# A bidirectional Mamba scan on one core: decays of the state pairs made further ahead, and projections moved to other steps

## The reference, cut to what matters

```
u, z = split(x @ in_w.T)
u    = silu(conv4(u) + conv_b)            # four taps over time
dbc  = u @ xproj_w.T
dt   = softplus(dbc[:, :64] @ dt_w.T + dt_b)
B, C = dbc[:, 64:80], dbc[:, 80:96]       # 16 states
A    = -exp(A_log)
h_n[t] = exp(dt[t] * A_n) * h_n[t-1] + dt[t] * u[t] * B_n[t]     # for each state n
y[t]   = sum over n of h_n[t] * C_n[t]  +  u[t] * D
out    = (y * silu(z)) @ out_w.T
```

## Time and profile before

| | us |
|---|---|
| median of 3 runs | 1427.17 (1426.55 to 1429.71) |
| the profiled execution | 1421.74 |
| its span | 1419.9 |
| busy: TensorE, VectorE, ScalarE, GpSimd | 1265.3, 1081.2, 966.3, 978.3 |
| TensorE's granted clock, mean | 0.987 of full speed |
| Mamba block, end of its last sum | about 870 |

### The profile page before, as it was taken

How to read it: one execution, slowest core, us unless ns; L and a number is a source line. 1 busy time by engine, 2 the same in 40 slices (tenths; PEclk the granted TensorE clock), 3 DMA queues, 4 the chain that set the end, 5 groups by cost and what they waited for, 6 DMA issues and landing times.

```text
span 1419.9 us, 28744 instructions
## 1 busy us (share of the span) xinstructions
PE 1265.3 (89%) x10310; PEld 977.1 (69%) x10310; DVE 1081.2 (76%) x1813; ACT 966.3 (68%) x1662; POOL 978.3 (69%) x604
## 2 busy tenths in 40 slices
PE   6698899899899898989989877998998999998995
PEld 2566766766677676676667765568997666666993
DVE  6688898888888988889888985433335788987775
ACT  5788887887878888888788794224555555454443
POOL 2688988898898898889889882621333466565673
PEclk9999999999999999999999989999999999999998
DMA  6544545445444544444544434231214200002233
GB/s 215 142 120 129 173 140 162 144 131 141 144 143 123 144 170 145 150 137 130 163 144 139 130 120 178 74 94 42 85 55 149 92 2 1 1 17 59 76 100 104
DMA packets 175036, 163.52 MB, mean 115 GB/s; under 512 B 114416, under 2 KB 139504, under 8 KB 165184
## 3 DMA queue, kind: packets, MB, share of 16 engines
q1 hardware_dynamic: 170128, 151.87, 34.8%
q0 software_dynamic: 4768, 9.81, 2.1%
HBM read 147.11 MB, written 20.52 MB: 118 GB/s over the span
## 4 chain that ended last, share of the span: by engine, by line
PE 60%; DVE 17%; ACT 12%; issue 8%; DMA 1%; POOL 1%; DVEq 1%; SPq 0%; POOLq 0%; ACTq 0%
DVE hh L900 9%; PE pa L511 9%; PE py L530 8%; PE pq L416 6%; ACT da L722 3%; PE bank L1591 2%; PE bank L1601 2%; PE bank L1587 2%; PE pr L2045 2%; PE pr L2248 2%; PE pr L2059 2%; PE bank L1507 2%; DVE hh L910 2%; PE pq L426 2%; PE pq L465 2%
## 5 line engine op out<-in xcount | busy, mean ns | idle before, releaser
L1065 POOL TENSOR_TENSOR hc<-hh,cs 128x1024 f32<-128x1024 f32 x256 | 598.1, 2370 | 116.3 <-DVE hh L900 107.4
L900 DVE TENSOR_TENSOR_SCAN hh<-da,st,pa 128x512 f32<-128x512 f32 x288 | 349.5, 1262 | 48.8 <-ACT da L722 29.2
L511 PE MATMUL pa<-dg,dtut 64*128 64x128 f32 x3072 | 236.3, 287 | 83.4 <-DVE hh L900 73.2
L511 PEld LDWEIGHTS pa<-dg,dtut 64*128 64x128 f32 x3072 | 201.0, 190 | 144.4 <-issue 138.5
L530 PE MATMUL py<-ident,hc 128*128 128x128 f32 x2048 | 271.9, 277 | 5.5 <-POOL hc L1065 3.1
L530 PEld LDWEIGHTS py<-ident,hc 128*128 128x128 f32 x2048 | 228.1, 142 | 53.3 <-issue 30.9
L722 ACT ACTIVATE da<-dt,w 128x512 f32<-128x512 f32 x384 | 251.5, 710 | 0.2
L900 DVE TENSOR_TENSOR_SCAN hh<-da,pa 128x512 f32<-128x512 f32 x96 | 111.5, 1205 | 25.3 <-PE pa L511 14.0
L416 PE MATMUL pq<-xn,w 128*128 128x512 f32 x248 | 124.2, 625 | 2.8 <-ACT xn L766 2.8
L910 DVE TENSOR_TENSOR_SCAN hh<-pa,st,hh 128x512 f32<-128x512 f32 x96 | 116.0, 1260 | 1.7 <-ACT pa L727 1.7
L1717 POOL DMA_INDIRECT ytoken<-ysort,token x39 | 39.9, 1023 | 103.1 <-ACT ysort L1649 102.5
(11 more groups left out here) (340 smaller groups left out, 2615.1 us busy)
## 6 DMA issues: line engine op xcount, KB each, us to landing
cs<-bcrows SPq DMA_DIRECT2D x64, 1024.0 KB, 5.0
dg<-blocks SPq DMA_DIRECT2D x96, 256.0 KB, 5.1
bs<-bcrows SPq DMA_DIRECT2D x32, 256.0 KB, 3.4
brow<-bcrows SPq DMA_DIRECT2D x32, 256.0 KB, 5.3
blocks<-bcrows SPq DMA_DIRECT2D x384, 1.0 KB, 3.2
xsorted<-in_pads SPq DMA_DIRECT2D x13, 387.0 KB, 6.3
rot<-in_rot SPq DMA_DIRECT2D x4, 1024.0 KB, 5.0
wx<-in_l_w SPq DMA_DIRECT2D x4, 1024.0 KB, 11.2
```

The costliest lines, as they stand in the source:

```text
L511: mm = pe.matmul(pa[i % SLOTS + r].rearrange("p (j k n) -> p k n j", n=2, k=4)[:, kt, :, :], dtut[rows, kt, h * P:(h + 1) * P], dg[k % DGS ...
L900: v.tensor_tensor_scan(hh[(NS * m + nj) % HHS][:, h, :], da[q % DAS][:, :], inflows, 0.0 if first else st[:, m % 2, nj, h:h + 1], ALU.mult ...
L1065: g.tensor_tensor(hc[s % HCS][:, :, :], hh[s % HHS][:, :, :], cs[j % 2][:, s % CG, :].unsqueeze(1).broadcast_to([P, HF, CH]), ALU.mult).th ...
```

## The change

The `da` ring gets eight tiles instead of six. The decays of the pairs are counted by a semaphore of their own, `s_da`, so that they may be made in another order than the other slots; it takes over the semaphore `s_zero` of a later phase, whose two waits there are raised by the 384 pair decays (`zero0 = UNITS * 4 * len(PAIRS)`; those lines are left out below). `elsewhere` therefore leaves the items "flow" out of the count of `s_slot`.

`DECAYS_FIRST` and `DECAYS_LATE` say at which step ScalarE makes which decays, ahead of or behind `prep`. dt is projected at steps 4 and 5 instead of 5 and 6, with its relu and abs at 5 and 6. The sigmoid comes at the end of step 6, the squares at 7, 8 and 10. The output projection of the late kind comes at steps 0 and 1 instead of 1 and 2. The taps of u go one each at steps 8 to 11 for half 0, and three at 12 and one at 13 for half 1; before they were two each at 10 to 13. `D * u` is made at step 5 and added with state 3, which is in step 7. The inflows at steps 10 and 11 stand ahead of the sum as in other steps.

```diff
--- before.py
+++ after.py
@@ -32,11 +32,13 @@
 BY_G = (0, 1)
 BY_V = (4, 13)
 SPREAD_AT = (0, 8)
+DECAYS_FIRST = {0: (1,), 1: (2, 3), 3: (4,), 6: (7,), 7: (10,), 8: (11,), 9: (12,), 11: (14,), 12: (13, 15), 15: (16,)}
+DECAYS_LATE = {4: (5, 6), 6: (8, 9)}
 BY_P = tuple(n for n in range(NS) if n not in BY_G + BY_V)
 PAIRS = tuple(BY_P[i:i + 2] for i in range(0, len(BY_P), 2))
 DGS = 3
 HQ = P // 2
-SLOTS, DAS, BG, BVS = 4, 6, 2, 2
+SLOTS, DAS, BG, BVS = 4, 8, 2, 2
 HHS, HCS = 6, 4
 LAG = 4
 
@@ -216,7 +219,7 @@
             s_slot, s_taken = sem("slot_filled"), sem("slot_taken")
             s_dtu = sem("dtu_made")
             s_b, s_db, s_gdb = sem("b_rows_in_psum"), sem("inflow_by_vector"), sem("inflow_by_gpsimd")
-            s_brow = s_back
+            s_brow, s_da = s_back, s_zero
             s_pin = sem("inflow_by_tensor")
             s_dout = sem("diagonals_out")
             s_dg = [sem(f"diagonals_in{i}") for i in range(DGS)]
@@ -303,11 +306,11 @@
 
                 handed_items = handed()
                 turn = {item: i for i, item in enumerate(handed_items)}
-                by_tensor = [item[0] == "y" for item in handed_items]
+                elsewhere = [item[0] in ("y", "flow") for item in handed_items]
 
                 def slot_count(i):
 
-                    return i + 1 - sum(by_tensor[:i + 1])
+                    return i + 1 - sum(elsewhere[:i + 1])
 
                 def dt_count(m):
 
@@ -381,7 +384,7 @@
 
                     return s // NS * len(by) + sum(n < s % NS for n in by)
 
-                DD_AT = 9
+                DD_AT = 3
                 EARLY = (13, 14, 15)
 
                 def turned_count(m, h):
@@ -472,17 +475,17 @@
                         if m < UNITS:
                             if n == 3:
                                 x_project(m)
-                            if n in (5, 6):
-                                dt_project(m, n - 5)
-                        if m >= 3 and late_out(m - 3) and n in (1, 2):
-                            out_project(m - 3, ((0, 1), (2, 3))[n - 1])
+                            if n in (4, 5):
+                                dt_project(m, n - 4)
+                        if m >= 3 and late_out(m - 3) and n in (0, 1):
+                            out_project(m - 3, ((0, 1), (2, 3))[n])
                         if m >= 2 and m - 2 < UNITS - 1 and not late_out(m - 2) and n in (8, 9):
                             out_project(m - 2, ((0, 1), (2, 3))[n - 8])
                         if m + 1 < UNITS:
-                            if n in (10, 11):
-                                u_half(m + 1, 0, ((0, 1), (2, 3))[n - 10])
+                            if n in (8, 9, 10, 11):
+                                u_half(m + 1, 0, (n - 8,))
                             if n in (12, 13):
-                                u_half(m + 1, 1, ((0, 1), (2, 3))[n - 12])
+                                u_half(m + 1, 1, ((0, 1, 2), (3,))[n - 12])
                         if m < UNITS and n in (14, 15):
                             z_half(m, n - 14)
 
@@ -574,7 +577,7 @@
                             turn_dtu(m, 1)
                         if n == NS - 1 and m + 1 < UNITS:
                             turn_dtu(m + 1, 0)
-                        if s + 1 < STEPS and by_pe(s + 1) and n not in (LAG + 1, 10, 11):
+                        if s + 1 < STEPS and by_pe(s + 1) and n != LAG + 1:
                             inflow(s + 1)
                         if s in (1, 2, 3):
                             pe.wait_ge(s_xt, s + 1)
@@ -590,8 +593,6 @@
                                 inflow(s + 1)
                         if n != LAG and s >= LAG:
                             add_up(s - LAG)
-                        if n in (10, 11):
-                            inflow(s + 1)
                         if n not in (LAG + 1, *EARLY):
                             prep(m + 1, n)
                     for s in range(STEPS - LAG, STEPS):
@@ -678,10 +679,8 @@
                         if m < UNITS:
                             if n == 4:
                                 keep_rows(m)
-                            if n in (6, 7):
-                                relu_abs(m, n - 6)
-                            if n == 7:
-                                sigmoid(m)
+                            if n in (5, 6):
+                                relu_abs(m, n - 5)
                         if m + 1 < UNITS and n == 14:
                             keep_pre(m + 1, 1)
                         if m < UNITS and n == 15:
@@ -690,11 +689,11 @@
                             keep_pre(m, 3)
                         if n == 1:
                             silu(m)
-                        if n == 12:
+                        if n == 5:
                             u_times_d(m - 1)
                         if m < UNITS:
-                            if n in (8, 9, 10):
-                                square(m, n - 8)
+                            if n in (7, 8, 10):
+                                square(m, (7, 8, 10).index(n))
                             if n == 11:
                                 relu_again(m)
                         if m + 1 < UNITS and n == 11:
@@ -719,7 +718,7 @@
                                     k0, j0 = (q - DAS) // 4, (q - DAS) % 4
                                     act.wait_ge(s_taken, turn["flow", k0, j0 // 2, j0 % 2] + 1)
                                 a = W_A + h * NS + PAIRS[k % len(PAIRS)][j]
-                                act.activation(da[q % DAS][:, :], dt[m % 2][:, h, :], ACT.Exp, scale=wd[m % 2][:, a:a + 1]).then_inc(s_slot, 1)
+                                act.activation(da[q % DAS][:, :], dt[m % 2][:, h, :], ACT.Exp, scale=wd[m % 2][:, a:a + 1]).then_inc(s_da, 1)
                         else:
                             for h in range(HF):
                                 i = turn["step", s, h]
@@ -802,13 +801,11 @@
                     for s in range(STEPS):
                         if s % NS == LAG and s >= NS:
                             keep_sum(s // NS - 1)
-                        ahead = s + 1 < STEPS and by_pe(s + 1) and BY_P.index((s + 1) % NS) % 2 and (s + 1) % NS < 10
-                        if s + 1 < STEPS and not ahead:
-                            decays(s + 1)
+                        for n in DECAYS_FIRST.get(s % NS, ()):
+                            if s // NS * NS + n < STEPS:
+                                decays(s // NS * NS + n)
                         if s == 0:
                             keep_dtu(0, 0)
-                        if s % NS == PAIRS[0][0] - 1:
-                            decays(s + 2)
                         if s >= 3 and s % 2:
                             keep_states(s - 3)
                         if s == 1:
@@ -821,14 +818,16 @@
                         if s == 4:
                             decay_rates(1)
                         prep(s // NS + 1, s % NS)
+                        for n in DECAYS_LATE.get(s % NS, ()):
+                            decays(s // NS * NS + n)
+                        if s % NS == 6 and s // NS + 1 < UNITS:
+                            sigmoid(s // NS + 1)
                         if s % NS == 0:
                             keep_dtu(s // NS, 1)
                         if s % NS in SPREAD_AT:
                             spread_b(s // NS * NS + BY_V[SPREAD_AT.index(s % NS)])
                         if s % NS == NS - 1 and s + 1 < STEPS:
                             keep_dtu(s // NS + 1, 0)
-                        if s % NS in [own[0] - 1 for own in PAIRS[1:] if own[1] < 10]:
-                            decays(s + 2)
                         if s // NS == UNITS - 1:
                             n = s % NS
                             if n == 1:
@@ -895,7 +894,7 @@
                             v.wait_ge(s_pin, 2 * k + h + 1)
                             for j, nj in enumerate(own):
                                 i, q = turn["flow", k, h, j], 4 * k + 2 * h + j
-                                v.wait_ge(s_slot, slot_count(i))
+                                v.wait_ge(s_da, q + 1)
                                 inflows = pa2[i // 2 % (SLOTS // 2)][:, j::2]
                                 v.tensor_tensor_scan(hh[(NS * m + nj) % HHS][:, h, :], da[q % DAS][:, :], inflows,
                                                      0.0 if first else st[:, m % 2, nj, h:h + 1], ALU.mult, ALU.add).then_inc(s_taken, 1)
...
```

More of the change, by code:

```diff
@@ L104, in build @@
         s_phase = sem("phase_done")
+        s_zero, zero0 = sem("pair_decayed_then_pad_zeroed"), UNITS * 4 * len(PAIRS)
         s_back = [sem(f"b_row_in_then_back_in{i}") for i in range(4)]
@@ L1231, in build @@
         s_ht, s_yo, s_ys = sem("hidden_made"), sem("y_made"), sem("y_kept")
-        s_zero = sem("pad_zeroed")
         routed = {"route": 0}
@@ L1652, in tiles_scalar @@
                     act.wait_ge(s_re, 32)
-                    act.wait_ge(s_zero, 1)
+                    act.wait_ge(s_zero, zero0 + 1)
                     kept_up(0)
```

(2 more changed lines are left out.)

## The result

The changed kernel took 1414.32 us in the median of 4 runs (1413.49 to 1416.28), the kernel before 1426.86 beside it: ratio 0.991, 95% interval 0.9893 to 0.9927. Forecast were 1386 and a range of 1368 to 1413. The direction was right; of the 41.5 us forecast, 12.5 came. The two profiled executions stand only 5.5 apart (1421.74 and 1416.28): units 1 to 14 took 12.6 us less (702.9 against 715.5), but unit 0 took 4.1 more and the part behind the last softplus 3.8 more (627.0 against 623.2). Those two parts vary by themselves. So the units are what can be compared.

The account below looks back on a forecast made before the run. VectorE was taken to pace the unit of 51.26 us, its waits falling from 5.85 to 2.7 (48.1 a unit). Gains of 44.3 less 2.8 for hand-overs gave 41.5 off 1427.17: 1386, range 1368 to 1413.

Parts of the forecast that it names:

- rival D: No gain: ScalarE's two chain loads each hold 1.4 longer, or a slot holds decays; 0.3 a unit left, 1422, chance 0.05.
- A: Half the gain: the wait behind dt's second half is 2.6, not 1.0; 1.5 a unit left, 1406, chance 0.19.
- What bounds the kernel: Unit of 51.26 us: VectorE paces, busy 45.4, with 5.85 of waits at five places; GpSimd follows, TensorE idles, then is late.
- States 11 to 15: TensorE's crowded stretch: inflow 15 comes earlier, its scans wait 0.7 instead of 1.45; bounds a gain of 0 to 1.45.
- Output projection: Moved to steps 0 and 1: VectorE's 2.02 wait goes, step 2 waits 0.5; net gain 1.2 to 2.02.
- dt one step earlier: Inflow 6 queues behind dt's second half on TensorE; step 6's scans wait 1.0 instead of 0.17; loss 0 to 3.45.
- C: Slower: inflow 6 hangs on a chain across three engines; abs 4 late costs 12 us, 1439, chance 0.10.
- Decays and sigmoid: ScalarE makes decays 7 to 9 before the sigmoid; step 9 and 10 waits of 1.91 and 0.30 go; net 1.2 to 2.2.
- Late next is TensorE: After the decay waits go, taps at steps 8 to 10 push inflow 11 to 45.55, wanted at 45.15: wait 0.4.
- Its eight tiles let it: Eight decay tiles allow the earlier decays: each waits for the pair two before, scanned at least 4 us earlier.
- D and the taps: D's 0.9 and three taps (2.9) at steps 7 to 10 hide in TensorE's slot waits of 4.6 a unit.
- The sum: Eleven units at 3.15, two at 2.8, small terms for units 0, 1, 15: 44.3, less 2.8 for hand-overs, 41.5.

Follow-up runs that it names:

- e1: Changed kernel with ScalarE copying states 4 and 5 ahead of the sigmoid and 6 and 7 ahead of step 9's decays; 1389.28 us, ratio 0.9761.
- e3: Changed kernel with earlier copies of states 4 to 7, and in step 11 the sum of state 7 ahead of inflow 12; 1379.88 us, ratio 0.9698.
- e10: Kernel before with only one part of the change: in step 11 the inflow of step 12 stands ahead of state 7's sum; 1445.47 us, ratio 1.0158.
- e4: e3 with dt's second half placed behind the inflow of step 6 in step 5 on TensorE; 1379.70 us, ratio 0.9693.
- e6: e3 with six decay tiles as before instead of eight; 1382.43 us, ratio 0.9691.
- e7: e3 with D times u made at step 12 and added with state 9, in step 13, as before; 1390.40 us, ratio 0.975.
- e5: e3 with the output projection back at steps 1 and 2; 1399.40 us, ratio 0.9797.
- e8: e3 plus 24 transposes of the unit matrix on TensorE in unit 0, step 4, ahead of the inflow; 1380.24 us, ratio 0.9677.
- e9: Changed kernel once more with no edit, on a further chip; 1410.93 us, ratio 0.9898.

## Why the prediction was wrong

Point by point, by its own steps. The sums hold, but for rival D, which by its own 0.3 a unit is 1423 and not 1422. The measured 1414.3 lies between A (1406) and D, and neither's mechanism was at work: the wait at step 6 was 1.43 and not 2.6, and the loads cost 1.28.

*What bounds the kernel* held: VectorE paces, and its five waits were the ones that moved.

*States 11 to 15* failed, and this is the second of two failed steps. The walk let inflow 12 go ahead of the sum of state 7 and counted that only as 1.0 us of TensorE's time in the crowded stretch, and took TensorE's durations from a unit whose clock was 1.00. The sum had filled part of the gap ahead of inflow 12, which was 1.15 to 1.20. Without it, behind a VectorE held by the copies, the gap was 1.85 to 1.98, and the clock fell: about 1.5 in each of eight units, 12 us. Even with the clock whole this order costs 0.61 a unit (e1 to e3). Put alone into the kernel before, it costs 21 us (e10). The wait for inflow 15 itself came out smaller than walked, 0.40 for 0.7.

*Output projection* held. The 2.02 went whole and inflow 2 gave back some 0.5. Undone, it costs 0.9 in a unit with whole clock, where a net gain of 1.2 to 2.02 had been set, and 14 to 19 us in all with the falls of the clock.

*dt one step earlier* held in its place, and roughly in its size (1.43, walked 1.0; 1.33 in unit 7), and so ScalarE's chain with loads of 1.28 did too. But as a loss it was oversized: taking the wait away (e4) gives only 0.17 a unit. Rivals A and C hung on this wait and were both wrong.

*Decays and sigmoid* is the step that failed first. "Late next is TensorE" holds only where nothing is copied (0.49 ahead of the scans of step 11 in unit 7, walked 0.4). In the eleven units with copies (1 to 5 and 8 to 13) late next was ScalarE itself. The step listed what ScalarE does from 31.2 to 46.8 and left out the copies of kept states, 0.19 us each, because they cost nothing as work. The rows could not show them: the walked unit, from 335.97 to 387.23, is unit 6, and from its own step 0 on nothing of it is copied. The unit before it, number 5, has the copies in the same trace. There the copy of the states 4 and 5, at 319.74, stands ahead of the sigmoid's load at 323.85, and nobody waits for any copy in the whole trace of before:

```profile
319.74 0.21 ACT L756 ACTIVATE st<-hh 128x4 f32<-128x4 f32 x1 [0.63 <-DVE hh L900]
322.56 0.69 ACT L645 ACTIVATE rx<-pq,w 128x512 f32<-128x512 f32 x1 [2.61 <-PE pq L443]
...
323.85 1.28 ACT L650 ACT_TABLE_LOAD   x1
```

Moving the sigmoid ahead of the odd step's copies put 5 us in front of them, and VectorE waited 2.1 and 0.35. "Its eight tiles let it" was not needed either (e6). With the copies moved (e1) units 1 to 14 take 24 us less, with the sum moved too (e3) 33.

*D and the taps* held in direction for D, worth 0.34 and not 0.9 (e7); the taps' share is not shown.

*The sum.* 14 units were to give 42.3 and gave 12.6 in the profiles. Unit 7, without copies and without a fall of the clock, gave 3.08 of the 3.15. With the copies alone moved (e1) they gave 36.6: a full unit 2.85, unit 1 1.3 for the 2.0 set, and unit 14 only 1.4 for 3.15. In unit 14 a second residual addition, at 756.11 in e1, waits 1.63 for its projection, a wait that is not there before; it is also the one wait of 1.6 that is left in the changed kernel's summary row for line 924. Unit 0 was to give 1.5 and took 4.1 more or 3.8 less in two profiles; no single profile can show a term of that size there. The 2.8 taken off for close hand-overs was no cover for a wait left out. With both causes taken away the kernel stands at 1379.9, 47.84 a unit against the 48.1 walked. That it lands near the forecast of 1386 is in part luck, as e3's order on TensorE is not the one that was walked.

## What to carry to other kernels

When instructions of an in-order engine are moved, list all that it issues behind them, the 0.2 us ones above all, and who waits for each: here a copy of 0.19 us held the pacing engine for 2.1. Take the rows from a unit that has all the work of the common case. When TensorE's work is taken out of a place where it waits, check how long the gap becomes and not only that the work fits elsewhere, since a longer gap can cost the clock as well. A ring need not be enlarged before the order shows that a slot is waited for.

## What the runs showed of the hardware

In units 1 to 14, each fall of TensorE's clock to its lower level of 1.2 GHz stood right behind a gap in its work, lasted about 3.4 us and made a full unit 1.5 to 1.7 us longer. The length of the gap alone does not settle it. Two gaps of 1.4 to 1.5 a unit did not do it in the one trace of the kernel before, where TensorE was idle 4.8 us a unit; one of 1.42 to 1.54 a unit did it in four of thirteen units of e5; gaps of 1.85 to 1.98 did it in eight of eleven units of the changed kernel, where a unit with whole clock has 3.2 idle, and of 2.02 to 2.08 in six of fourteen of e10. With no gap above 1.24 us (e1 to e4, e6 to e8) it never fell in units 1 to 14. Which of equal gaps it follows changed from one execution to the next (e9). Other executions of the kernel before had a lower mean clock (0.975 to 0.986, against 0.987 in the trace) and have no trace, so whether it falls in the units there is open.

A load of ScalarE's function table held ScalarE for 1.28 us: the next instruction began within 0.02 of its end (224.38 behind the load of 223.09, 226.85 behind that of 225.55).
